# Four graph layers on one core: f32 key rows for the graph attention, and a weighted one-hot in one operation per tile

## What is computed

```python
    # graph attention, twice (8 heads, then 1)
    scores = leaky_relu(s_src[src] + s_trg[trg] + s_tp, 0.2)
    exp_s = jnp.exp(scores - jnp.max(scores))
    denom = jax.ops.segment_sum(exp_s, trg, num_segments=N)[trg]
    out = jax.ops.segment_sum(proj[src] * (exp_s / (denom + 1e-16))[:, :, None], trg, num_segments=N)
    ...
    # filter
    weights = decay * gate                      # one per edge
    messages = weights[:, None] * x[sender]
    agg = jax.ops.segment_sum(messages, receiver, num_segments=n_nodes)
    agg = agg / jnp.maximum(degree, 1.0)[:, None]
    return x + agg @ W_mix
```

## Time and profile before

| | us |
|---|---|
| median of 3 runs (6353.58 to 6361.06) | 6356.11 |
| the profiled execution | 6354.84 |
| its span | 6353.2 |
| PE / DVE / ACT / POOL busy | 3334.9 / 3706.0 / 1197.1 / 3176.5 |
| first attention pass, gathers' first to last start | 2088.7 to 2642.6 |
| second attention pass, the same | 2754.7 to 3291.8 |
| filter pass, the same | 5754.3 to 6303.2 |

### The profile page before, as it was taken

One profiled execution on the slowest core, in us unless ns is written; L12 is line 12 of the kernel. 1 busy time (PEld: TensorE's weight loads), 2 busy tenths in 40 slices (PEclk: granted clock), 3 DMA queues, 4 the chain that ended last, 5 costly groups with the idle time before them and its releaser, 6 DMA issues. The chain is left out here.

```text
span 6353.2 us, 88104 instructions
## 1 busy us (share of the span) xinstructions
PE 3334.9 (52%) x20818; PEld 2497.8 (39%) x20821; DVE 3706.0 (58%) x13503; ACT 1197.1 (19%) x3916; POOL 3176.5 (50%) x3375
## 2 busy tenths in 40 slices
PE   1000110015663566446655897887986888932333
PEld 0000010004442455335543554554565777732333
DVE  9200830039995677757776646447356888874444
ACT  0000000004552111111110000000004889920000
POOL 2777177735772677457750460640733700005775
PEclk9999999997886555555556897898898999975555
DMA  7000000005662333233334776666633744401112
GB/s 295 3 3 3 23 3 3 3 13 144 186 187 82 83 77 76 46 67 76 78 50 88 154 170 130 147 151 138 164 82 90 199 116 116 114 17 48 50 50 45
DMA packets 929367, 567.19 MB, mean 89 GB/s; under 512 B 598770, under 2 KB 873436, under 8 KB 925148
## 3 DMA queue, kind: packets, MB, share of 16 engines
q1 hardware_dynamic: 811868, 351.32, 22.4%
q0 software_dynamic: 117248, 212.96, 14.3%
HBM read 384.62 MB, written 179.43 MB: 89 GB/s over the span
## 5 line engine op out<-in xcount | busy, mean ns | idle before, releaser
L802 POOL DMA_INDIRECT fild_g<-table,fild_ring x416 | 423.6, 1018 | 787.0 <-ACT fild_ring L816 662.7
L246 POOL DMA_INDIRECT recordsS<-sortS_rS,sortS_addrS x416 | 425.4, 1023 | 263.3 <-DVE sortS_addrS L287 136.9
L802 POOL DMA_INDIRECT gatAp_g<-table_heads,gatAp_ring x416 | 428.4, 1030 | 249.2 <-issue 124.0
L802 POOL DMA_INDIRECT gatBp_g<-table_head,gatBp_ring x416 | 411.6, 989 | 237.6 <-issue 124.3
L246 POOL DMA_INDIRECT recordsD<-sortD_rD,sortD_addrD x392 | 401.2, 1023 | 221.8 <-issue 119.1
L866 PE MATMUL fild_ps<-fild_g,fild_oh 128*128 128x128 f32 x832 | 213.2, 438 | 391.8 <-DMA fild_g<-table,fild_ring 306.0
L762 PE MATMUL pairs_p_b<-pairs_blk,pairs_oh 128*128 128x256 f16 x1024 | 289.9, 310 | 177.9 <-DVE pairs_oh L749 174.4
L866 PEld LDWEIGHTS fild_ps<-fild_g,fild_oh 128*128 128x128 f32 x832 | 185.2, 327 | 419.7 <-issue 183.8
L777 ACT CAST pairs_blk<-pairs_p_b 128x512 f16<-128x512 f32 x512 | 284.0, 588 | 215.0 <-PE pairs_p_b L764 209.2
L155 POOL DMA_INDIRECT gcn0e_held_attr<-in_edge_attr,recD x160 | 157.4, 984 | 312.0 <-POOLq L86 263.6
L155 POOL DMA_INDIRECT gcn2e_held_attr<-in_edge_attr,indexS x160 | 157.4, 984 | 259.4 <-POOLq L86 211.1
(11 more groups left out here) (662 smaller groups left out, 10641.9 us busy)
## 6 DMA issues: line engine op xcount, KB each, us to landing
gcnw_strip<-pairs SPq DMA_DIRECT2D x150, 800.0 KB, 6.4
pairs<-pairs_blk SPq DMA_DIRECT2D x768, 64.0 KB
pairs<-sortD_blank SPq DMA_DIRECT2D x27, 1600.0 KB, 37.9
attD_g<-attrD SPq DMA_DIRECT2D x104, 256.0 KB
attS_g<-attrS SPq DMA_DIRECT2D x104, 256.0 KB, 3.7
pairs<-pairs_blk POOLq DMA_DIRECT2D x256, 64.0 KB, 2.6
gatAp_rowb<-locD SPq DMA_DIRECT2D x104, 128.0 KB, 3.0
gatBp_rowb<-locD SPq DMA_DIRECT2D x104, 128.0 KB
```

The costliest lines, as they stand in the source:

```text
L246: pool.indirect_dma_start(self.rec_dram, bass.IndirectOffsetOnAxis(ap=self.addr[:, c:c + 1], axis=0), self.r[:, c, :], None, bounds_check= ...
L802: pool.indirect_dma_start(rows(u, k), None, table, bass.IndirectOffsetOnAxis(ap=ring[:, u, k:k + 1], axis=0)).then_inc(gathered[u], 16)
```

## The change

The kernel gets a second DRAM table of the turned keys, in f32 (`C.loc32`). At the end of the first sort, VectorE copies each piece out of PSUM twice, and SP stores both. The attention passes load their key rows from the f32 table, so that a group's load has twice the bytes and the compare an f32 input; its result stays bf16. In the filter, four operations per group, one per tile, compare with the key and multiply by the weight at once; the key and the weight are per-partition scalars. The semaphore between the two old operations is gone.

```diff
--- before.py
+++ after.py
@@ -333,6 +333,7 @@
         blank = ph.sb("blank", [P, NT * 2 * P], F16)
         p_tr = ph.ps("p_tr", [P, 4, P])
         loct = ph.sb("loct", [P, len(TR), P], BF16)
+        loct32 = ph.sb("loct32", [P, len(TR), P])
         filled, loaded, blanked, tr_ready, tr_done, loc_stored = (
             ph.sem(x) for x in ("filled", "loaded", "blanked", "tr_ready", "tr_done", "loc_stored"))
         block = ph.block()
@@ -352,7 +353,8 @@
             sp.wait_ge(tr_done, 1)
             for k, (t, n) in enumerate(TR):
                 sp.dma_start(C.loc["D"][t:t + n, :], loct[0:n, k, :]).then_inc(loc_stored, 16)
-            sp.wait_ge(loc_stored, 16 * len(TR))
+                sp.dma_start(C.loc32[t:t + n, :], loct32[0:n, k, :]).then_inc(loc_stored, 16)
+            sp.wait_ge(loc_stored, 2 * 16 * len(TR))
 
         @block.gpsimd
         def _(pool):
@@ -390,6 +392,7 @@
             j.match_low(V, dve)
             dve.wait_ge(tr_ready, 1)
             for k, (t, n) in enumerate(TR):
+                nc.vector.tensor_copy(loct32[0:n, k, :], p_tr[0:n, k, :])
                 last = nc.vector.tensor_copy(loct[0:n, k, :], p_tr[0:n, k, :])
             last.then_inc(tr_done, 1)
 
@@ -876,8 +879,8 @@
         oh = ph.sb("oh", [P, U, G, P])
         ring = ph.sb("ring", [P, U, G], I32)
         ps = [ph.ps(f"ps{u % 2}", [P, G, 256]) for u in range(2)] * (U // 2)
-        indexed, oh_ready, raw_ready, acc_done, acc_set, squared = (
-            ph.sem(x) for x in ("indexed", "oh_ready", "raw_ready", "acc_done", "acc_set", "squared"))
+        indexed, oh_ready, acc_done, acc_set, squared = (
+            ph.sem(x) for x in ("indexed", "oh_ready", "acc_done", "acc_set", "squared"))
         gathered = [ph.sem(f"gathered{u}") for u in range(U)]
         block = ph.block()
 
@@ -912,10 +915,11 @@
                 if weights is None:
                     one_hot(nc, C, side, oh[:, u], i, u).then_inc(oh_ready, 1)
                     return
-                one_hot(nc, C, side, oh[:, u], i, u).then_inc(raw_ready, 1)
-                dve.wait_ge(raw_ready, nth(i, u))
-                w = weights[:, tiles(i, u)].unsqueeze(2).to_broadcast([P, G, P])
-                nc.vector.tensor_tensor(oh[:, u], oh[:, u], w, ALU.mult).then_inc(oh_ready, 1)
+                for k in range(G):
+                    t = i * (U * G) + u * G + k
+                    last = nc.vector.tensor_scalar(oh[:, u, k, :], C.iota_row[:], C.rec[side][:, bass.ds(t, 1), 1],
+                                                   weights[:, bass.ds(t, 1)], ALU.is_equal, ALU.mult)
+                last.then_inc(oh_ready, 1)
 
             def step(i, u, before=U, left=U):
                 if left:
@@ -951,7 +955,7 @@
         msg = ph.sb("msg", [P, U, G, W])
         oh = ph.sb("oh", [P, U, G, P])
         oht = ph.sb("oht", [P, U, GS], BF16)
-        rowb = ph.sb("rowb", [P, U, GS], BF16)
+        rowb = ph.sb("rowb", [P, U, GS])
         ring = ph.sb("ring", [P, U, G], I32)
         z = ph.sb("z", [P, U, G, H])
         rm = ph.sb("rm", [P, 1])
@@ -977,7 +981,7 @@
 
         @block.sync
         def _(sp):
-            load_key_rows(sp, C.loc["D"], rowb, rows_loaded, oht_ready)
+            load_key_rows(sp, C.loc32, rowb, rows_loaded, oht_ready)
 
         @block.vector
         def _(dve):
@@ -2223,6 +2227,7 @@
             C.cnt[s] = sb(f"cnt{s}", [P, NT])
             C.loc[s] = nc.dram_tensor(f"loc{s}", [T, P], BF16).ap()
             records[s] = nc.dram_tensor(f"records{s}", [SLOTS, RW], F32).ap()
+        C.loc32 = nc.dram_tensor("loc32", [T, P], F32).ap()
         C.rec["D"] = sb("recD", [P, T, RW])
         index_s = sb("indexS", [P, T], I32)
         C.index["D"], C.index["S"] = C.rec["D"][:, :, 4].bitcast(I32), index_s[:]
```

## The result

| | before | changed |
|---|---|---|
| median of 4 runs, us | 6355.72 | 6305.66 (6303.24 to 6307.49) |
| ratio, 95% interval | | 0.992 [0.9903, 0.9937] |
| the profiled execution, its span | 6354.84, 6353.2 | 6307.49, 6305.9 |

What follows compares the result with a forecast made beforehand. GpSimd's issue of 416 gathers was taken to bound each gather pass. Filter -24, attention 0 and sort +2.6 gave -21.4 us on 6354.84, so 6333 us, range 6320 to 6348.

Steps and rivals of the forecast that it cites:

- Bound and mechanism: Filter and attention passes: GpSimd's 416 gathers set the length; a VectorE operation running at a gather's start holds it.
- One that starts later does not: All gather passes: a VectorE operation that starts after a gather has started does not hold that gather.
- Filter: Filter pass: four short operations replace compare and multiply, cutting gather holds for a gain of 24 us, ends 12 to 28.
- I take 4 us left: Filter: holds remaining from the new operations, priced at random points, 0.04 us per group times 104, out of 28.0.
- my two bounds: Filter: each new operation, with two per-partition scalars, was bounded by 0.285 and 0.35 us; 0.285 was taken.
- I take **0** for both passes together: Attention: holds freed and holds made by the longer match cancel; net 0, ends 17 us each way.
- The price of L997: Attention: the transposed match (L993 before the change) on f32 rows takes 0.487 us instead of 0.346.
- The formula for random places: Attention: an operation of length d costs (d - 0.13)^2 / 2 / 1.32 us; 26 us per pass before, 29 after.
- the netting: Attention: a shift by the longer match frees holds here and makes others there, so the sum was set to 0.
- Attention shrinks: Rival, first attention pass: holds vanish and don't come back, 15 us less, giving 6318 us; chance 0.06.
- Sort: End of the first sort: four more PSUM copies and four more stores add 2.6 us, ends 1.7 and 4.
- The mid-gather rival: Rival, filter: new operations also hold GpSimd mid-gather, 30 us replacing the 28 that go, so no gain; chance 0.06.

Runs made afterwards that it cites:

- e1: Kernel before with only the new four-operation filter, attention keeping bf16 key rows: 6320.86 us against 6348.58, ratio 0.9961.
- e3: Kernel before, bf16 key rows kept, with two one-column VectorE copies behind the transposed match in both attention passes: 6328.91 us against 6348.58.
- e5: Kernel before with the filter's compare and multiply each cut into four two-input 128x128 operations, semaphore kept: 6322.90 us against 6349.50.
- e4: Kernel before with each bf16 key row loaded a second time into a buffer nothing reads, both waited for: 6346.53 us.
- e2: Kernel before with only the f32 key table, its stores and loads, and the old filter: ratio 0.9977.
- e6: Changed kernel with one unused f32 copy of 128x1024 behind the four one-hot operations of each filter group: 6327.68 us against 6349.50.
- e7: Changed kernel with both sorts' low-bits match made by one 128x128 one-input operation per column: 6269.0 us, ratio 0.9875.
- e12: Kernel before with four one-column VectorE copies behind the transposed match in both attention passes: 6428.66 us against 6349.24.
- e13: e12 with 32 one-column copies, run once, ahead of the loop of the edge attention's first pass: 6351.82 us against 6335.46.
- e10: e7 with both attention passes' compare and messages each split into four 128x128 operations: 6329.62 us, ratio 0.9966.

## Why the prediction was wrong

- **Bound and mechanism: right.** GpSimd sets the length of all three passes, and what VectorE does to it is, nearly all, holds at a gather's start. e1, e3 and e5 show it three ways, and of the 121 lengthened gathers of the first pass before the change, 117 lose the running operation's end less 0.13 us, within 0.02; they make up 35.5 us. "One that starts later does not" is too wide: 30 gathers of the changed kernel lose 2.3 us to an L997 that starts inside them.
- **Filter: nearly right.** "I take 4 us left": 0.8 are left, and the gain was 27.5 us instead of 24, inside its ends. 82 gathers start while an L920 runs, nearly one per group as priced, but for 63 of them the operation has too little left (under 0.14 us) to cost anything; I had named a steady distance between a landing and the build and still priced random points. The new operation takes 342 ns, not 285. It has two per-partition scalars, and the second adds about as much (57 ns) as I had read for the first (60) from the earlier trace rows. It cost nothing, being hidden, and I had taken the wrong one of my two bounds.
- **Attention: the step that failed.** "I take **0** for both passes together": it was -17. The price of L997 (487 predicted, 479 measured), the hidden extra work and the harmless loads (e4) all held. The formula for random places did not: it gives 29 us of holds per pass after the change, and 17.8 and 18.2 were measured. What failed was the netting: I let what the earlier trace rows showed be cancelled by holds made elsewhere, on no evidence. The positions aren't random. 33 of 104 compares stood in the 0.25 us ahead of a gather and cost 16.0 us; 27 of them (13.1 us) came directly behind a match that a gather had delayed and that ended at a fixed point, 1.06 us behind that gather's start. With f32 rows the shift of 0.13 us moves that cluster past the start (1 is left, 2 in e2); in e3, 0.12 us leaves 24 there, with 8.2 us. What moved in elsewhere was smaller: the compares' holds fell by 11.0 us in all. The messages' fell by another 9.6, which neither nor the prediction had. I had the outcome as a rival, "Attention shrinks", at 0.06, with -15 us. With the measured -17 and the filter's 27.5 the sum is 6354.8 - 27.5 - 17 + 2.4 = 6312.7. The 5.6 us from untouched stages make up the rest, and no term was forecast for them; single runs of the kernel before differ by more.
- **Second pass.** It stayed at 411 in three kernels with f32 rows (410.9; e6 410.8; e7 411.0) and rose by 3 in e2. Only 10 of its compares stood ahead of a gather, so the shift had 4.8 us to win there and not 16.0; those 4.8 came back at other places (all compares hold 7.8 us against 7.0), the messages' holds fell from 11.9 to 9.5, and other operations' rose by 1. Why e3 came down to 406.2 wasn't followed.
- **Sort: right.** 2.6 predicted, 2.4 measured.
- **The mid-gather rival: false in the filter**, where I had put it, but not as a mechanism: L997 does it in attention, for 2.3 us in both passes. The earlier trace rows couldn't decide it: that L993 ended 0.79 us into its gather, just ahead of the 0.82 from which e6 shows a loss. The L997 of 0.479 us can end later, which I hadn't asked.
- **Range.** The two ends I had written down, 28 us for the filter and 17 for attention, give 6354.8 - 28 - 17 + 2.6 = 6312.4 together; the range stopped at 6320. The measured 6305.66 lies below both.

## What to carry over

Where GpSimd's issue of indirect DMAs sets the pace, look at the length of each single VectorE operation beside it, not at their sum: four of 0.3 us are better than one of 0.7, even if they add up to more. Before netting a shift to zero, count where the starts of the long operations stand relative to the gathers; a cluster just ahead of them can make a small delay a gain. Here 0.12 to 0.13 us brought the first pass to about 411 us, and twice that left it at 414.9 and 422.1. And after each change that makes a loop's code longer, look at the instruction queue's packets per stage, in untouched stages too.

## What the hardware did that I had not expected

- A one-input copy of 0.68 us that starts 0.43 to 0.71 us inside a gather holds it by its end less 0.82 us (e6), and so does the f32 match of 0.48 us in the changed kernel (20 gathers, 1.8 us). One that starts later doesn't hold that gather, and may be lengthened itself: the 24 matches that start 0.474 to 0.607 us inside all end at 1.19. Scalar operations of 0.34 us held nothing in the middle of a gather.
- A loop of the same code ran 456.3 or 373.5 us by its place alone, with 61 or 12 packets of 8 KB on the instruction queue (e12, e13); in e10 `attS` took 447.4 instead of 369.2.
- A scalar operation of 128x128 in f32 takes 226 ns with no per-partition scalar, 285 with one and 342 with two.
